# A graph layer on one core: GpSimd's stops between gathers, one in four instead of one in two in the later blocks

## The chip, the core and the metric

The kernel runs on one core of a Trainium2 chip. The core has a matrix engine (TensorE, PE in the profile), a vector engine (VectorE, DVE), a scalar engine (ScalarE, ACT), GpSimd (POOL) and a queue engine (SyncE, SP). They run at the same time and wait for each other by semaphores. Sixteen DMA engines move data between the main memory (HBM) and the on-chip memory (SBUF). The metric is the device time of one execution in microseconds (us), less is better.

## The reference, cut to what matters

```python
def gnn(h, src, dst, rel, norm, bases, w_comp):      # 6250 nodes x 256, 200000 edges sorted by dst, 32 relations, 8 bases
    weight = einsum('rb,bio->rio', w_comp, bases)
    xw = einsum('ni,rio->nro', h, weight)
    msg = xw[src, rel] * norm                        # one row of 256 per edge
    return relu(segment_sum(msg, dst))

def mix(x, ...):      # linear attention over all nodes: K'V summed over all, then per node
    ...               # msg = Q KV Z, @ Wm, layernorm, concat with x, @ W1, relu, @ W2, layernorm, x + msg

def ffn(x, ...):      # 8 experts, all of them for every node, weighted by a softmax router
    ...               # per expert: relu(bn(x W1)), relu(bn(h W2)), h Wo; sum_e w_e y_e

xn = layernorm(x)
x = x + gnn(xn, ...) + mix(xn, ...)
out = x + ffn(layernorm(x), ...)
```

## The kernel before, in words

**The edge part.** The 200000 edges are cut into chunks of 128 (one per partition). A *step* takes one chunk: a gather brings the 128 source rows of 256 floats from `normed_nodes` (`xnD`) into one of the 16 slots of a ring in SBUF, and TensorE multiplies the slot by a selection matrix (`steps(...)` on GpSimd issues the gather, `step(it, k)` on TensorE multiplies: four matmuls of 128x128 per step, tile `PS<-steps`). VectorE adds each step's product to the running sums (line 1433), and SyncE stores them four steps at a time to `step_sums` in HBM (line 546). Sixteen steps make an *iteration*; there are 123 of them, 1968 steps and so 1968 gathers. In the trace all tensors carved from the big buffer are called `steps`.

**The ring.** The gather for a slot may start once TensorE has done the step that used the slot 16 steps earlier: GpSimd waits on `mm_done`. TensorE waits, in front of every even step, on `row_in`, which counts the landing of that step's and the next step's gather, and on `acc_done`, which tells that VectorE has taken the sums two steps back.

**The stretches.** Iterations 0 to 16 carry the first mix pass (keys, values, queries, the first half of W1 for three node tiles of 128 each). Four iterations have steps only. Then three tiles of the second mix pass take two iterations each, and from iteration 27 on the work is cut into *blocks* of eight iterations. Block 0 has steps, the second mix pass for the next block's tiles (`mixing`) and the combination of step sums with the bases (`combine`, matmuls `PS<-bases_s,feed`). Blocks 1 to 11 have these and the eight experts for the tiles of the block before (`first`, `second`, `third`: `PS<-x1t_high,split_in` and the like). After the last step the experts of the last tiles run alone.

**The order of work.** Each engine's program is written out by hand; at each step number fixed pieces of mixing, combining and expert work stand between the steps. TensorE, VectorE and ScalarE take them strictly in that order, so TensorE that waits for a gather holds up all that stands behind it. The eight reads of step sums that a tile's combination needs (`load_agg`, line 576) are issued by SyncE behind the stores of the iteration before; ScalarE reorders them (line 993) for TensorE.

**GpSimd's stops.** GpSimd's only work in the steady stretches is the gathers. In front of some it stops: it writes a small tile `hold` (`memset`, line 796) and waits on the semaphore `held` until that write is done, and only then issues the gather (line 798). Two constants say where:

```python
CALM_END, LIGHT_END = 16, 36
```

In iterations 0 to 15 and 36 to 122 it stops in front of every second gather (16 x 8 + 87 x 8 = 824 stops); in iterations 16 to 35 it never does. Iteration 36 is the second of block 1.

Of the kernel before, what the change touches and what calls it, by code (L numbers as in the profile page):

```python
# [55 lines left out]
UN = 16  # L56
# [24 lines left out]
SETS = 4  # L81
# [8 lines left out]
CALM_END, LIGHT_END = 16, 36  # L90
# [14 lines left out]
def gps_layer(nc, x, src, dst, etype, eweight, bases, w_comp, Wq, Wk, Wv, Wm, W1, W2, g1, b1, g2, b2,  # L105
              Wr, br, fW1, fb1, fg1, fbe1, fm1, fv1, fW2, fb2, fg2, fbe2, fm2, fv2, Wo, bo, out):
    ctx = ExitStack()
    with ctx:
        sems = {}

        def sem(name):
            if name not in sems:
                sems[name] = ctx.enter_context(nc.semaphore(name))
            return sems[name]
# [257 lines left out]
        def wait_apart(eng, name, value):  # L372


            eng.wait_ge(sem(name), value)
            eng.sem_inc(sem("passed"), 1)
# [360 lines left out]
        def _(pool):  # L737
# [50 lines left out]
            pool.wait_ge(sem("rels_out1"), 16)  # L788
            pool.wait_ge(sem("ln_st"), 16 * (LG + 1))

            def steps(it, u, calm=None):
                pool.wait_ge(sem("idx_ready"), it + 1)
                for k in range(UN):
                    wait_apart(pool, "mm_done", it * UN + k + 1)
                    if calm is not None and k % 2 == 0:
                        pool.memset(hold[:, :], 0.0).then_inc(sem("held"), 1)  # L796
                        wait_apart(pool, "held", calm * (UN // 2) + k // 2 + 1)
                    pool.indirect_dma_start(out=ring[:, k, :], out_offset=None, in_=xnD,  # L798
                                            in_offset=bass.IndirectOffsetOnAxis(ap=idxc[:, u, k:k + 1], axis=0)
                                            ).then_inc(sem(f"row_in{k // 2}"), 16)  # L800

            for it in range(ITERS):
                if it < CALM_END:
                    steps(it, it % SETS, it)
                elif it < LIGHT_END:
                    steps(it, it % SETS)
                else:
                    steps(it, it % SETS, it - LIGHT_END + CALM_END)

        @block.scalar  # L810
        def _(act):
# [1430 lines left out]
```

## Time and profile before

| | us |
| --- | --- |
| median of 3 runs | 3474.31 |
| lowest, highest | 3462.02, 3476.06 |
| the profiled execution | 3473.02 |
| its span, first to last instruction | 3471.2 |
| mean granted TensorE clock | 0.947 |
| PE busy | 2978.8 (86%) |
| DVE busy | 2236.0 (64%) |
| POOL busy | 2061.6 (59%) |
| ACT busy | 1001.9 (29%) |

Busy is the time in which an engine executed something of the program; waits and the handling between instructions are not in it. The profile names for each idle stretch what ended it ("<-"); "issue" means that it saw nothing that ended it. GpSimd's spans are rough, so its pace is better read from one start to the next.

### The profile page before, as it was taken

Reading aid. Unit: us, or ns where it says so; the run is one execution under the profiler, and the core shown is the slowest. Engines: PE = TensorE matmul, PEld = TensorE weight load, DVE = VectorE, ACT = ScalarE, POOL = GpSimd, SP = SyncE. Lnnn points to the kernel's source line nnn. Section 1 sums busy time; section 2 is a strip of 40 time slices with the busy share of each in tenths; the row PEclk is TensorE's granted clock in tenths of the full one; section 3 lists DMA queues with packets and bytes.
Section 4 is the critical chain, followed back from the end, with each engine's and each line's share of the span. In section 5 each row is a group of like instructions: output and inputs, shape, how many; then the busy total and the mean of one; then the engine's idle time right before and its main releaser. Section 6 shows DMA issues by size and latency. Waiting matters only on the chain.

```text
span 3471.2 us, 60187 instructions
## 1 busy us (share of the span) xinstructions
PE 2978.8 (86%) x17948; PEld 2616.7 (75%) x17948; DVE 2236.0 (64%) x5966; ACT 1001.9 (29%) x1702; POOL 2061.6 (59%) x2827
## 2 busy tenths in 40 slices
PE   0599996565769989999999999999999999999888
PEld 0477875555658878888887888878888888878778
DVE  4566666455557767777677776766767676767633
ACT  0433331000103333233333333333333333323244
POOL 1466666666566666666666666666666666666600
PEclk9999998678879999999999999999999999999999
DMA  7799987666668888787888878888887888878744
GB/s 179 246 295 294 297 290 234 204 190 201 204 206 267 256 261 266 239 274 244 264 258 258 267 241 266 254 260 255 260 265 247 263 256 268 266 239 274 228 151 144
DMA packets 638070, 852.74 MB, mean 246 GB/s; under 512 B 63579, under 2 KB 515497, under 8 KB 637607
## 3 DMA queue, kind: packets, MB, share of 16 engines
q1 hardware_dynamic: 495087, 536.50, 47.9%
q0 software_dynamic: 95776, 262.27, 26.2%
q10 hardware_dynamic: 46872, 50.02, 4.3%
q8 instruction: 147, 2.41, 0.3%
q14 instruction: 188, 1.54, 0.1%
HBM read 542.52 MB, written 314.58 MB: 247 GB/s over the span
## 4 chain that ended last, share of the span: by engine, by line
PE 58%; issue 13%; DVE 11%; DMA 6%; POOL 4%; another core or an unknown queue 4%; ACTq 2%; ACT 1%; DVEq 0%; SPq 0%; POOLq 0%; PEld 0%; PEldq 0%
PE PS L1850 57%; DMA steps<-normed_nodes,steps 5%; DVE steps L1433 4%; POOL steps L798 4%; DVE h_low L1096 1%; PE PS L1920 1%; DVE feed L1096 1%; DVE steps L1387 1%; ACTq L815 1%; DMA step_sums<-steps 0%; DVE feed L1764 0%; ACT feed L852 0%; DVE steps L1151 0%; POOL hold L796 0%
## 5 line engine op out<-in xcount | busy, mean ns | idle before, releaser
L798 POOL DMA_INDIRECT steps<-normed_nodes,steps x1968 | 1942.1, 987 | 1122.3 <-issue 566.5
L1433 DVE SCALAR_TENSOR_TENSOR steps<-steps,PS 128x256 f32<-128x256 f32 x1968 | 942.5, 479 | 839.7 <-PE PS L1850 478.7
L1850 PE MATMUL PS<-steps 128*128 128x128 f32 x7872 | 1201.3, 291 | 270.3 <-issue 107.1
L1850 PEld LDWEIGHTS PS<-steps 128*128 128x128 f32 x7872 | 1106.2, 203 | 369.3 <-issue 270.9
L1850 PE MATMUL PS<-bases_s,feed 128*128 128x256 f32 x1568 | 370.0, 379 | 2.3 <-issue 2.3
L986 ACT ACTIVATE feed<-PS,bnc 128x512 f32<-128x512 f32 (+1 forms) x416 | 307.4, 751 | 173.4 <-PE PS L1850 141.8
L1387 DVE TENSOR_TENSOR steps<-steps 128x512 f32<-128x512 f32 x495 | 330.0, 687 | 4.3
L1850 PEld LDWEIGHTS PS<-bases_s,feed 128*128 128x128 f32 x1568 | 286.6, 190 | 37.6 <-issue 3.1
L1850 PE MATMUL PS<-w_one,feed 128*128 128x256 f32 (+1 forms) x980 | 295.1, 433 | 2.2 <-issue 2.2
L985 ACT ACTIVATE h_high<-PS,bnc 128x512 fp32r<-128x512 f32 (+1 forms) x208 | 156.7, 753 | 453.1 <-PE PS L1850 313.3
L993 ACT COPY feed<-feed 128x1024 f32<-128x1024 f32 x98 | 205.4, 2096 | 198.0 <-DMA feed<-step_sums 169.2
L1850 PE MATMUL PS<-h_high,split_in 128*128 128x512 f32 (+1 forms) x832 | 247.7, 421 | 11.2 <-ACT feed L986 11.2
L1850 PE MATMUL PS<-x1t_high,split_in 128*128 128x512 f32 (+1 forms) x832 | 236.4, 406 | 0.0
L1850 PEld LDWEIGHTS PS<-w_one,feed 128*128 128x128 f32 x980 | 175.1, 194 | 43.0 <-issue 30.0
L1850 PE MATMUL PS<-w_zero,feed 128*128 128x256 f32 x784 | 196.6, 386 | 4.0 <-DVE feed L1096 3.5
L1764 DVE SCALAR_TENSOR_TENSOR feed<-PS,rw,feed 128x256 f32<-128x256 f32 x392 | 169.8, 475 | 31.7 <-PE PS L1850 31.5
L943 ACT COPY mixbuf<-PS 128x256 f32<-128x256 f32 x49 | 18.3, 373 | 578.5 <-issue 267.2
L1850 PEld LDWEIGHTS PS<-h_high,split_in 128*128 128x128 f32 x832 | 149.2, 199 | 35.1 <-ACT feed L986 13.7
L1850 PEld LDWEIGHTS PS<-feed,w_one 128*128 128x128 f32 x1176 | 149.4, 194 | 27.3 <-issue 27.3
L1096 DVE TENSOR_TENSOR h_low<-feed,h_high 128x512 fp32r<-128x512 f32 (+1 forms) x208 | 129.1, 656 | 48.5 <-ACT feed L986 48.5
L1850 PE MATMUL PS<-feed,w_one 128*128 128x128 f32 x1176 | 157.5, 277 | 0.7 <-issue 0.7
L1850 PEld LDWEIGHTS PS<-x1t_high,split_in 128*128 128x128 f32 x832 | 144.0, 192 | 15.7
(229 smaller groups left out, 2959.4 us busy)
## 6 DMA issues: line engine op xcount, KB each, us to landing
step_sums<-steps SPq DMA_DIRECT2D x492, 512.0 KB
split_in<-expert_split SPq DMA_DIRECT2D x104, 1024.0 KB
feed<-step_sums SPq DMA_DIRECT2D x392, 128.0 KB
steps<-step_types SPq DMA_DIRECT2D x126, 256.0 KB
steps<-normed_nodes,steps POOLq DMA_INDIRECT x1968
w_zero<-in_L_ffn_Wo_dram SPq DMA_DIRECT2D x52, 256.0 KB
w_one<-in_L_ffn_Wo_dram SPq DMA_DIRECT2D x52, 256.0 KB
mixbuf<-mix_hidden SPq DMA_DIRECT2D x50, 256.0 KB
```

The costliest lines, as they stand in the source:

```text
L798: pool.indirect_dma_start(out=ring[:, k, :], out_offset=None, in_=xnD, in_offset=bass.IndirectOffsetOnAxis(ap=idxc[:, u, k:k + 1], axis=0) ...
L815: act.dma_start(lnx[g][:, 0:LT, :], x[nodes_at(g), :].rearrange("(t p) n -> p t n", p=P)).then_inc(sem(f"ln_ld{g}"), 16)
L943: act.copy(mst[:, :, :].rearrange("p k n -> p (k n)"), bank(B_MIX, 0, C)).then_inc(sem("m2_mt"), 1)
L985: act.activation(h1_high[:, k, 0:w], bank(b0 + k, 0, w), ACT.Relu, bias=bias, scale=scale)
L986: act.activation(o[:, k, 0:w], bank(b0 + k, 0, w), ACT.Relu, bias=bias, scale=scale).then_inc(sem(f"f_h{s}"), 1)
L993: act.copy(agg[:, h, :, :], at_nodes[:, h, :, :]).then_inc(sem("b_agg"), 1)
L1096: return dve.tensor_tensor(o, a, b, op)
L1387: dve.tensor_tensor(selm[:, q, :, :, :], hot[:, s, :].unsqueeze(3).to_broadcast([P, BATCH, GN, BASES]), coef[:, s, :].unsqueeze(2).to_broa ...
L1433: dve.scalar_tensor_tensor(acc[:, k % ACCR, :], acc[:, (k - 1) % ACCR, :], keepc[:, k:k + 1], PS[:, a:a + C], ALU.mult, ALU.add).then_inc( ...
L1764: dve.scalar_tensor_tensor(oacc[:, j, :], o_part(j), rw[:, EXPERTS * j + e:EXPERTS * j + e + 1], oacc[:, j, :], ALU.mult, ALU.add).then_in ...
L1850: return pe.matmul(o, a, b, start=start, stop=stop)
L1920: last = pe.transpose(o[:, h * P:(h + 1) * P], frm[:, h * P:(h + 1) * P], ident[:, :])
```

## The change

`steps` on GpSimd gets the distance between two stops as an argument, and the count of stops made before the iteration as another. Iterations 0 to 15 keep a stop in front of every second gather, iterations 16 to 35 keep none, and iterations 36 to 122 now have one in front of every fourth: 16 x 8 + 87 x 4 = 476 stops.

```diff
-            def steps(it, u, calm=None):
+            def steps(it, u, calm=None, apart=2):
                 pool.wait_ge(sem("idx_ready"), it + 1)
                 for k in range(UN):
                     wait_apart(pool, "mm_done", it * UN + k + 1)
-                    if calm is not None and k % 2 == 0:
+                    if calm is not None and k % apart == 0:
                         pool.memset(hold[:, :], 0.0).then_inc(sem("held"), 1)
-                        wait_apart(pool, "held", calm * (UN // 2) + k // 2 + 1)
+                        wait_apart(pool, "held", calm + k // apart + 1)
...
                 if it < CALM_END:
-                    steps(it, it % SETS, it)
+                    steps(it, it % SETS, it * (UN // 2))
                 elif it < LIGHT_END:
                     steps(it, it % SETS)
                 else:
-                    steps(it, it % SETS, it - LIGHT_END + CALM_END)
+                    steps(it, it % SETS, CALM_END * (UN // 2) + (it - LIGHT_END) * (UN // 4), 4)
```

On GpSimd, where iteration 35 goes over into 36, the order before is this (the first line holds the last two gathers of iteration 15 and the 320 of iterations 16 to 35):

```order
L798 DMA steps<-normed_nodes,steps 128x256 x322
L796 MEMSET hold 128x8
L798 DMA steps<-normed_nodes,steps 128x256 x2
L796 MEMSET hold 128x8
L798 DMA steps<-normed_nodes,steps 128x256 x2
L796 MEMSET hold 128x8
```

and after the change, at the same place:

```order
L798 DMA steps<-normed_nodes,steps 128x256 x322
L796 MEMSET hold 128x8
L798 DMA steps<-normed_nodes,steps 128x256 x4
L796 MEMSET hold 128x8
L798 DMA steps<-normed_nodes,steps 128x256 x4
L796 MEMSET hold 128x8
```

What moved: every second `hold` of this stretch is gone, nothing else.

On GpSimd within the blocks, with what each instruction waits for, around the start of an iteration (the wait on `idx_ready`), before:

```order
L798 DMA steps<-normed_nodes,steps 128x256 [waits mm_done]
L796 MEMSET hold 128x8 [waits mm_done]
L798 DMA steps<-normed_nodes,steps 128x256 [waits held]
L798 DMA steps<-normed_nodes,steps 128x256 [waits mm_done]
L796 MEMSET hold 128x8 [waits idx_ready,mm_done]
L798 DMA steps<-normed_nodes,steps 128x256 [waits held]
```

and after:

```order
L796 MEMSET hold 128x8 [waits mm_done]
L798 DMA steps<-normed_nodes,steps 128x256 [waits held]
L798 DMA steps<-normed_nodes,steps 128x256 [waits mm_done] x3
L796 MEMSET hold 128x8 [waits idx_ready,mm_done]
L798 DMA steps<-normed_nodes,steps 128x256 [waits held]
```

What moved: of four gathers, three now wait for `mm_done` alone and one for `held`, where it was two and two. The instructions of TensorE, VectorE, ScalarE and SyncE stand in the same order as before.

## Rows read from the trace of the kernel before

**Rows 1.** Busy time by stretch; columns as in the first line.
```profile
core 0: us, PE busy (x) PEld busy (x) DVE busy (x) ACT busy (x) POOL busy (x), PEclk, DMA share, GB/s
200.00:600.00 400.00, 345.14 (x2423) 293.46 (x2422) 251.90 (x586) 114.88 (x351) 256.09 (x351) 0.94 0.87 282
1100.00:1220.00 120.00, 115.28 (x733) 105.47 (x732) 88.45 (x254) 37.54 (x62) 78.35 (x111) 0.99 0.84 264
1240.00:1280.00 40.00, 34.03 (x191) 28.92 (x190) 28.99 (x84) 14.84 (x20) 25.11 (x38) 0.93 0.87 279
1280.00:1380.00 100.00, 97.52 (x584) 86.64 (x582) 66.68 (x183) 32.31 (x44) 65.47 (x94) 1.00 0.85 262
1284.00:2929.00 1645.00, 1563.22 (x9348) 1371.37 (x9347) 1154.63 (x3126) 529.30 (x755) 1069.44 (x1531) 0.98 0.83 258
3300.00:3471.00 171.00, 146.15 (x721) 130.94 (x719) 54.62 (x142) 76.52 (x114) 0.00 (x0) 0.96 0.46 148
```

**Rows 2.** GpSimd's groups, 1284 to 2929 us.
```profile
L798 POOL DMA_INDIRECT steps<-normed_nodes,steps x1021 | 1008.2, 987 | 576.1 <-issue 300.7 <-PE PS L1850 168.9 <-POOL hold L796 103.8
L796 POOL MEMSET hold<- 128x8 f32 x510 | 62.8, 123 | 0.2
```

**Rows 3.** GpSimd in order of time, in a block: start, us, what.
```profile
2006.80 0.95 POOL L798 DMA_INDIRECT steps<-normed_nodes,steps  x1 [0.79 <-issue]
2008.06 0.95 POOL L798 DMA_INDIRECT steps<-normed_nodes,steps  x1 [0.30 <-issue]
2009.01 0.12 POOL L796 MEMSET hold<- 128x8 f32 x1
2009.91 0.95 POOL L798 DMA_INDIRECT steps<-normed_nodes,steps  x1 [0.79 <-POOL hold L796]
```

**Rows 4.** GpSimd in order of time, in the stretch without stops.
```profile
702.05 0.95 POOL L798 DMA_INDIRECT steps<-normed_nodes,steps  x1 [2.71 <-PE PS L1850]
703.30 0.95 POOL L798 DMA_INDIRECT steps<-normed_nodes,steps  x1 [0.30 <-issue]
704.56 0.94 POOL L798 DMA_INDIRECT steps<-normed_nodes,steps  x1 [0.30 <-issue]
705.80 0.95 POOL L798 DMA_INDIRECT steps<-normed_nodes,steps  x1 [0.30 <-PE PS L1850]
```

**Rows 5.** TensorE's groups, 1284 to 2929 us.
```profile
L1850 PE MATMUL PS<-steps 128*128 128x128 f32 x4084 | 596.5, 281 | 70.0 <-issue 32.8 <-DMA steps<-normed_nodes,steps 26.9 <-DVE steps L1433 8.4
L1850 PE MATMUL PS<-bases_s,feed 128*128 128x256 f32 x1020 | 241.2, 379 | 0.0
```

**Rows 6.** GpSimd and TensorE in order of time, around one stop of TensorE.
```profile
1241.07 0.95 POOL L798 DMA_INDIRECT steps<-normed_nodes,steps  x1 [0.79 <-POOL hold L796]
1242.32 0.94 POOL L798 DMA_INDIRECT steps<-normed_nodes,steps  x1 [0.30 <-issue]
...
1244.09 0.52 PEld L1850 LDWEIGHTS PS<-steps 128*128 128x128 f32 x4 [3.04 <-issue]
1244.12 0.68 PE L1850 MATMUL PS<-steps 128*128 128x128 f32 x4 [2.67 <-issue]
```

**Rows 7.** TensorE's groups, 1100 to 1220 us.
```profile
L1850 PE MATMUL PS<-steps 128*128 128x128 f32 x334 | 48.9, 282 | 3.3 <-DVE steps L1433 2.3 <-issue 1.0
```

**Rows 8.** Waits of ScalarE: us in total, times, longest; 1898 to 3134 us.
```profile
ACT feed L993 <- DMA feed<-step_sums: 65.6, 13, 11.1
```

**Rows 9.** The same in block 0, 837 to 1050 us.
```profile
ACT feed L993 <- DMA feed<-step_sums: 19.4, 2, 14.2
```

**Rows 10.** Clock and DMA by slices of the span (40 equal ones), from the page.
```profile
PEclk9999998678879999999999999999999999999999
DMA  7799987666668888787888878888887888878744
```

## The prediction

> **What bounds the kernel now.** I read the slices of the page first, then busy time by stretch, then GpSimd alone, and last what TensorE stops for. The slices show that the clock sags only between slices 7 and 12, which the change doesn't touch, and is at 9 in all the blocks, with the DMA engines at 7 to 8 tenths [rows 10]. So the change acts in a stretch that looks full of TensorE work. From 1284 to 2929 us, which is eight blocks, TensorE is busy for 1563.22 of 1645 us: 205.6 us a block, 195.4 of them busy, 10.2 idle [rows 1].
>
> GpSimd looks idle there (1069.44 of 1645 us), and isn't. Its 1021 gathers take 1008.2 us, its 510 stops 62.8, and 576.1 us of idle time stand in front of gathers [rows 2]. In order of time this idle time is two fixed pieces: 0.30 us in front of a gather without a stop, 0.79 behind a stop, whatever releaser is named [rows 3]. Half the gathers have each: 510 x (0.79 + 0.30) = 556 us. Of 1645 us only 576 - 556 = 20 are left in which GpSimd waited for somebody, 1.2%. So `mm_done`, the ring's own brake, hardly ever holds it: it issues at its own pace, and that pace is the blocks' pace. A pair of gathers takes 2009.91 - 2006.80 = 3.11 us, 64 pairs take 199 us, and with the longer ones (mean 987 ns against the usual 950) and the 20 us it comes to 205.6.
>
> TensorE pays for it in front of steps: 70.0 us of its 81.8 idle us stand before the matmuls `PS<-steps`, 26.9 put down to the gather's DMA, 32.8 to "issue", 8.4 to VectorE [rows 5]. I count "issue" as gathers too, from the stop at 1244: the two gathers that this step needs were issued at 1241.07 and 1242.32 and ended on GpSimd at 1243.26, and the weights are loaded 0.83 us later, after 3.04 us of idle time for which no releaser is named [rows 6]. So 59.7 us in 1645 are waits for a gather, 3.6%.
>
> The counterproof is the beginning of block 1, where the stretch without stops has left GpSimd ahead: from 1100 to 1220 us the idle time before steps is 3.3 us, none of it put down to a gather and most to VectorE [rows 7].
>
> **The change, part by part.** It removes 87 x 4 = 348 stops from iterations 36 to 122. Each takes 0.12 us for the write and 0.79 - 0.30 = 0.49 us more of idle time, 0.61 us together [rows 3]. That gathers without stops follow each other at the short distance is seen directly, 703.30 to 704.56 to 705.80, 1.25 us [rows 4]. So four gathers take 2 x 3.11 - 0.61 = 5.61 us in place of 6.22, an iteration loses 4 x 0.61 = 2.4 us of GpSimd time and a block 19.5. GpSimd's own pace becomes 205.6 - 19.5 = 186 us a block, and 348 x 0.61 = 212 us of its time go in all. None of this is yet the kernel's time: 186 us lie below TensorE's 195.4 busy us, so TensorE becomes what is late, and only its stops can be won.
>
> Term 1, the stops. GpSimd still has its lead at 1220 us [rows 7], TensorE stops for gathers from 1240 on [rows 6], and the steps end at about 3300, as GpSimd's empty last stretch shows [rows 1]: 2080 us from 1220, of which 3.63% (59.7 / 1645) are waits for gathers, 75 us. With 9 us a block to spare, 16 slots are refilled after a slow gather, and the waits should go nearly all. Bounds: 0 if the waits are of another kind than I take them for, -75 if all go. I take -75, because GpSimd's spare time is larger than the waits.
>
> Term 2, the clock. After a cluster of stops TensorE's granted clock falls from its upper level (2.4 GHz) to its lower (1.2): the stretch 1240 to 1280, with 6 us idle, has 0.93, the one behind it, with 2.5 in 100, has 1.00 [rows 1]. A mean of 0.98 in the blocks means 4% of the time at the lower level, 83 us of 2080. At most half of it, 42 us, is lost work. Part of these falls come without a gather's stop, and not all work scales with the clock. Bounds 0 and -42, and I take -10, near the lower one. The Trainium skill, TensorE: Matmul & The Clock Gate, Part 1, says that the throttled state is the default and activity releases it. The trace agrees in the direction (0.93 beside 1.00). By the rule taken strictly, blocks without stops stay at 1.00, and this term is the whole of it; that is the third rival.
>
> Term 3, what comes to light. A stop for a gather also gives VectorE and ScalarE time to catch up. Where GpSimd was ahead, from 1100 to 1220, TensorE was still idle for 4.72 of 120 us, 3.9% [rows 1], half of it before steps on VectorE's sums [rows 7]. In the steady blocks the idle time that is not a gather's is 81.8 - 59.7 = 22.1 us, 1.3%. If it rises to 3.9%, 2.6% of 2080 us come back, 54 us. Bounds 0 and +54. Block 1 follows a disturbed stretch and is one sample, so I take half, +27.
>
> The stops in iterations 0 to 15 stay, and nothing upstream of iteration 36 changes: 0. The removed write goes to a tile of 128x8 that nobody reads: 0. The tail after 3300 us is TensorE and ScalarE alone and has no gathers: 0. No DMA is added or removed, they only come up to 5% denser, which is the second rival.
>
> Sum: -75 - 10 + 27 = -58 us. Against the profiled execution's 3473.0 us (span 3471.2 and 1.8 around it) that is 3415 us. The median of the runs shown, 3474.3, is 1.3 above the profiled one, so I leave it at 3415, 1.7% less than before. By the ends of the terms the range of this case is 3473 - 117 = 3356 to 3473 - 21 = 3452.
>
> **The rivals.**
>
> The first: the stops go, but other waits take their place, and the time stays, 3466 us (3456 to 3490). The hand-written order has hops through VectorE and ScalarE (`mixing`, line 1433, the experts' hidden rows) that are timed by TensorE's passing; term 3 is then at its full 54, the clock gives nothing, and some 15 us of gather waits stay: -75 + 15 + 54 = -6. For it speaks block 1, where an idle share of 3.9% stood with no gather late. Against it: the blocks from 1284 on have only 1.3% of such idle time. That the change doesn't do what it says ends here too: if the freed 0.49 us were not idle time but the descriptor work of the gather before, GpSimd's pace would stay and so would the time. The 1.25 us between gathers without stops [rows 4] speak against that.
>
> The second, on the other side: transfers collide, 3520 us. The place is the read of the step sums for a tile's combination. ScalarE already waits for it, 65.6 us in 13 waits in six blocks of 24 tiles, the longest 11.1 [rows 8], and in block 0, without stops, 19.4 us in only two waits, the longest 14.2 [rows 9]. TensorE has cover today: 0.0 us idle before `PS<-bases_s,feed` [rows 5]. With gathers issued in longer runs beside stores and reads, at a DMA share of 0.83 in the blocks where the first mix pass has 0.87 [rows 1], these reads land later; once the cover is used up, each us per tile costs 43 us over the 43 tiles of blocks 1 to 11. At 2.5 us a tile it is 107, less the 58 won: +49, 3522. It decides from 1.4 us a tile beyond the cover, and shows as slower from 1.8. Against it: once the ring is full, gathers are issued at TensorE's pace, not in longer runs. The Trainium skill, DMA: Bandwidth & Descriptors, Queues, rings and completion order, says that each DMA engine takes turns between its queues by packets, which would let a run of gathers push SyncE's reads back. No row here shows the turns themselves, only the share of 0.83.
>
> The third: the clock stays up and nothing comes to light, -75 - 42 = -117, 3356 us. For it: the stretch at 1280 to 1380 with 2.5% idle and a clock of 1.00. Against it: such stretches are short, and in block 1 TensorE stops for VectorE though no gather is late [rows 7].
>
> **How the numbers follow.** The forecast has 0.47, the third rival 0.11, the first 0.23, the second 0.19. What a measurement of this kernel can tell from no change is about 0.5%, 17 us, so 3457 to 3491 is the same. The forecast and the third rival are faster, and 0.02 of the first at its lower edge: 0.60. Same is 0.22, with the rest of the first and a little of the second. Slower is 0.18. The range must reach up into the second rival for its cheaper half and down to the third: 3350 to 3500 leaves out some 0.05 below and 0.11 above. The forecast's own range is 3356 to 3452.
>
> **What would show it.** In the profile of the changed kernel: 476 stops on line 796; GpSimd's idle time before gathers in the blocks with waits of 1 us and more for TensorE, a sign that the ring is full; the idle time before `PS<-steps` from 70 us in eight blocks to under 25, with VectorE's line 1433 as its first releaser; a block in about 200 us in place of 205.6; the clock in the blocks at 0.99. Wrong I am if blocks still take 205 us: with the idle time before steps gone and other idle time in its place it is the first rival, with ScalarE's waits on `feed<-step_sums` doubled and idle time before `PS<-bases_s,feed` the second, and with GpSimd still never waiting its pace was not what I took it for.

## The result, and the profile after

| | before | changed |
| --- | --- | --- |
| median, us | 3471.32 (4 runs, 3462.02 to 3476.06) | 3606.15 (4 runs, 3586.7 to 3614.09) |
| profiled execution's span | 3471.2 | 3584.9 |
| mean granted TensorE clock | 0.947 | 0.937 |
| POOL busy | 2061.6 | 2017.8 |
| stops | 824 | 476 |

The changed kernel is slower: 1.0376 of before, 95% interval 1.0347 to 1.0406. The forecast was 3415 us with a range of 3350 to 3500, so the sign is wrong and the time lies outside the range. The profiled execution of the changed kernel was the fastest of its four: the two spans differ by 113.7 us, the medians by 134.8.

The page after: the clock by slices [rows 10], the chain that ended last, and the group of the steps on TensorE.

```profile
PEclk9999997677879999999999999999999999999999
PE 64%; DVE 13%; issue 10%; another core or an unknown queue 7%; DMA 2%; ACT 2%; ACTq 2%; POOL 1%; SPq 1%; DVEq 0%; POOLq 0%; PEld 0%; PEldq 0%
L1850 PE MATMUL PS<-steps 128*128 128x128 f32 x7872 | 1211.0, 292 | 259.9 <-DVE steps L1433 158.9
```

The clock sags in the same slices as before. Where TensorE stops in front of steps, it now waits for VectorE, not for gathers. The chain has 7% of "another core or an unknown queue" in a program that runs on one core. Time by stretch: iterations 16 to 35, and eight whole blocks (from the first step of block 2).

```profile
core 0: us, PE busy (x) PEld busy (x) DVE busy (x) ACT busy (x) POOL busy (x), PEclk, DMA share, GB/s
567.70:1075.40 507.70, 328.99 (x1818) 297.08 (x1818) 292.44 (x759) 47.12 (x85) 311.72 (x324) 0.76 0.69 203
1263.20:3001.40 1738.20, 1593.72 (x9378) 1392.41 (x9377) 1161.25 (x3134) 532.14 (x760) 1036.15 (x1277) 0.97 0.78 245
```

The same eight blocks of before, cut at the same instructions, and of GpSimd and TensorE the groups in the eight blocks after, which answer to [rows 2, 5]:

```profile
1244.10:2895.00 1650.90, 1570.24 (x9377) 1377.81 (x9377) 1157.73 (x3132) 533.62 (x760) 1072.50 (x1535) 0.98 0.82 258
L1850 PE MATMUL PS<-steps 128*128 128x128 f32 x4097 | 598.9, 282 | 72.5 <-issue 33.5 <-DMA steps<-normed_nodes,steps 27.4 <-DVE steps L1433 9.7
```

```profile
L796 POOL MEMSET hold<- 128x8 f32 x256 | 30.0, 117 | 105.3 <-issue 71.4 <-PE PS L1850 30.5 <-remote 3.0
L1850 PE MATMUL PS<-steps 128*128 128x128 f32 x4097 | 602.9, 283 | 59.2 <-DVE steps L1433 49.5 <-issue 8.7
L1850 PE MATMUL PS<-bases_s,feed 128*128 128x256 f32 x1024 | 243.1, 380 | 0.3 <-issue 0.3
L1850 PE MATMUL PS<-h_low,split_in 128*128 128x512 f32 x256 | 103.1, 454 | 38.7 <-issue 19.3 <-DVE h_low L1096 14.7
L1850 PE MATMUL PS<-w_s,mixbuf 128*128 128x256 f32 x257 | 66.8, 405 | 24.0 <-ACT mixbuf L961 23.9
L1850 PE MATMUL PS<-wm_s,mixbuf 128*128 128x256 f32 x128 | 34.6, 393 | 10.8 <-issue 10.0 <-ACT mixbuf L943 0.6
```

A block takes 1738.2 / 8 = 217.3 us, before 206.4. GpSimd does what was foretold: in front of `hold` it now waits 105.3 us (before 0.2), so the ring is full, and of TensorE's 60.9 us of gather waits (33.5 + 27.4, with "issue" counted as gathers) some 9 are left. But TensorE is idle for 144.5 us against 80.7, in front of steps on VectorE's sums (49.5 against 9.7), on `h_low` (before 4.8), `w_s` (0.6) and `wm_s` (0.9).

Why these come late shows in the waits of the other engines. Those put down to "remote", a releaser that the profile doesn't see, of 5 us or more in the eight blocks:

```profile
ACT h_high L985 <- remote: 58.6, 12, 8.1
DVE steps L1433 <- remote: 51.3, 18, 5.0
ACT feed L986 <- remote: 49.7, 21, 4.1
ACT mixbuf L955 <- remote: 49.1, 15, 4.2
ACT feed L1001 <- remote: 44.1, 8, 6.1
DVE mixbuf L1096 <- remote: 39.8, 8, 7.3
ACT mixbuf L943 <- remote: 30.5, 3, 11.7
POOL steps L798 <- remote: 30.0, 22, 2.0
DVE feed L1764 <- remote: 9.6, 9, 2.0
```

With the small ones they are 371 us; in the same blocks of before 43 (23.8 of it at L943 and 11.3 at L1433). These are whole waits, summed over three engines that can wait at the same time; they are not lateness alone, and not time of the kernel. Nearly all of these instructions wait for a semaphore of TensorE. One case in order of time, start and length:

```profile
1570.85 1.14 PE L1850 MATMUL PS<-steps 128*128 128x128 f32 x8
1571.83 0.38 PE L1920 MATMUL PS<-ident,mixbuf 128*128 128x128 f32 x2
1572.05 1.06 PE L1850 MATMUL PS<-steps 128*128 128x128 f32 x8
1572.86 1.18 PE L1850 MATMUL PS<-h_high,split_in 128*128 128x512 f32 x4
1574.76 0.95 POOL L798 DMA_INDIRECT steps<-normed_nodes,steps  x1 [0.79 <-issue]
1574.88 0.99 DVE L1433 SCALAR_TENSOR_TENSOR steps<-steps,PS 128x256 f32<-128x256 f32 x2 [3.20 <-remote]
1574.92 0.81 ACT L955 ACTIVATE mixbuf<-PS,gb 128x128 f32<-128x128 f32 x2 [3.22 <-remote]
1575.79 1.29 DVE L1096 TENSOR_TENSOR h_low<-feed,h_high 128x512 fp32r<-128x512 f32 x2
1576.53 0.80 PE L1850 MATMUL PS<-h_low,split_in 128*128 128x512 f32 x1 [2.49 <-issue]
```

VectorE waits for the first group of step products, which ends at 1571.99, and ScalarE for the transposes, which end at 1572.21. Both start at 1574.9, 2.9 and 2.7 us later, though TensorE itself had gone on to the next steps and to `h_high` at once. The trace also keeps when each semaphore was updated: for these two it has 1574.86 and 1574.90, just before the two engines start. Then VectorE's `h_low` is late, and TensorE stands for 2.49 us. The Trainium skill, Perfetto Trace Analysis, Tensor Engine Instruction (MATMUL, LD_WEIGHTS), says that the end shown for a matmul is estimated, and that its semaphore is pushed only after PSUM (the memory that matmuls write to) has acknowledged the write and seen by others later still; a bar can so be over while its semaphore is not yet out. The trace agrees: the update stands 2.87 us behind the end of the bar here, and 0.01 us at the same place in the second group's trace.

So the trace shows TensorE's work seen late. It doesn't show why. It has a second oddity: of the 1968 updates of the steps' semaphore it holds 1540, and the first trace of before 1332; between 1572.00 and 1574.86 it has none by any engine, not even that of `hold`, though GpSimd passed its wait on it at 1574.01. With updates missing, the sums under "remote" are no full account. Starts and ends of instructions are, and they are counted below.

The first question was whether the change brings this on every chip.

### The profile page after: what moved, and what is told of

It reads as the page before. It is cut to its first block, busy times and chain, and to the rows that moved or that the text cites. A ratio compares the mean times of both kernels' runs of the same rounds, so it can differ in the third digit from the quotient of the medians.

```text
span 3584.9 us, 59491 instructions
## 1 busy us (share of the span) xinstructions
PE 3017.8 (84%) x17948; PEld 2646.3 (74%) x17948; DVE 2241.9 (63%) x5966; ACT 999.8 (28%) x1702; POOL 2017.8 (56%) x2479
## 4 chain that ended last, share of the span: by engine, by line
PE 64%; DVE 13%; issue 10%; another core or an unknown queue 7%; DMA 2%; ACT 2%; ACTq 2%; POOL 1%; SPq 1%; DVEq 0%; POOLq 0%; PEld 0%; PEldq 0%
PE PS L1850 62%; DVE steps L1433 5%; DVE h_low L1096 2%; PE PS L1920 1%; DMA steps<-normed_nodes,steps 1%; DVE steps L1387 1%; POOL steps L798 1%; DVE feed L1764 1%; ACTq L815 1%; DVE feed L1096 1%; SPq L576 0%; PE PS L1958 0%; DMA feed<-step_sums 0%; ACT h_high L985 0%
## 5 line engine op out<-in xcount | busy, mean ns | idle before, releaser
L1433 DVE SCALAR_TENSOR_TENSOR steps<-steps,PS 128x256 f32<-128x256 f32 x1968 | 943.1, 479 | 904.6 <-PE PS L1850 601.4
L1850 PEld LDWEIGHTS PS<-steps 128*128 128x128 f32 x7872 | 1121.2, 205 | 343.7 <-issue 296.1
L1850 PE MATMUL PS<-w_one,feed 128*128 128x256 f32 (+1 forms) x980 | 303.4, 443 | 2.2 <-issue 2.2
L1850 PE MATMUL PS<-h_low,split_in 128*128 128x512 f32 (+1 forms) x416 | 156.6, 434 | 53.6 <-issue 24.6
L943 ACT COPY mixbuf<-PS 128x256 f32<-128x256 f32 x49 | 18.3, 373 | 612.2 <-PE PS L1920 314.1
L1850 PEld LDWEIGHTS PS<-h_low,split_in 128*128 128x128 f32 x416 | 82.8, 200 | 110.0 <-DVE h_low L1096 62.1
```

Of the source, the lines that this page charges most:

```text
L943: act.copy(mst[:, :, :].rearrange("p k n -> p (k n)"), bank(B_MIX, 0, C)).then_inc(sem("m2_mt"), 1)
L1433: dve.scalar_tensor_tensor(acc[:, k % ACCR, :], acc[:, (k - 1) % ACCR, :], keepc[:, k:k + 1], PS[:, a:a + C], ALU.mult, ALU.add).then_inc( ...
L1850: return pe.matmul(o, a, b, start=start, stop=stop)
```

## The experiments

The runs came to four chips, one for each group below; each group has its own runs of before, 7 in number. The results carry the numbers of these four, but not of the chip of the first measurement. I call that one the first chip; that it is a fifth, and not one of the four in another state, rests on its times alone.

### First group: the stops alone

Three theories. *Run*: lateness (of a semaphore behind the end of its matmul) grows with the gathers that GpSimd issues behind one another. *Ring*: what counts is that GpSimd catches up and waits on TensorE. *Chain*: the first rival of the prediction, the order's hops through VectorE and ScalarE. All edits are in the call of `steps` for iterations 36 on (`times=2` makes each stop twice; `near` lets a gather start only that many steps later, so that it is 6 steps ahead of TensorE and not 16):

```diff
four_two_stops:  steps(it, it % SETS, 4, times=2)
two_near:        steps(it, it % SETS, 2, near=10)
none:            steps(it, it % SETS, 0)
everywhere:      steps(it, it % SETS, 2)     # and in iterations 16 to 35 too
```

**four_two_stops.** 

> The changed kernel (a stop in front of every fourth gather in iterations 36 to 122), but each of these stops is made twice in a row, so that GpSimd's own pace is again about that of before (5.6 us for four gathers plus some 0.6 to 0.9 for the second stop, against 6.2 before) and it hardly ever waits for the ring. The symptom in the changed kernel is that VectorE, ScalarE and GpSimd together see TensorE's semaphore some us after its matmul (waits of these engines that the profile puts down to 'remote'). Theory run: this comes from four gathers in a row without a stop between them; then it stays here, with 'remote' waits of VectorE's line 1433 at 20 us and more in eight blocks, and a time of 3530 to 3620 us. Theory ring: it comes from GpSimd standing at its wait for TensorE because the ring is full; then it is gone, with the time at 3460 to 3500 us. Theory chain: there is no late semaphore, TensorE's other waits only came to light when the gathers were early; then the time is that of before too, 3460 to 3500, since the gathers are as late as before.

**two_near.** 

> The kernel before (a stop in front of every second gather), but in iterations 36 to 122 a gather may start only when TensorE has done the step 6 before it in place of 16 before it: GpSimd then often waits for TensorE, in runs of two gathers at most. Theory run: no late semaphores; the time rises only by the smaller buffer, which catches less of TensorE's unevenness: 3500 to 3600 us, idle time of TensorE before steps put down to gathers, 'remote' waits of line 1433 as small as before (about 10 us in eight blocks). Theory ring: the late semaphores come here too, 'remote' waits of line 1433 at 20 us and more in eight blocks. The time alone does not tell the two apart, the releasers do.

**none.** 

> No stop at all in iterations 36 to 122 (the first mix pass keeps every second): the dose. Theory run: longer runs, later semaphores, clearly slower than the changed kernel, 3650 to 3850 us, 'remote' waits larger than in it. Theory ring: the ring is full as in the changed kernel, so about its time, 3590 to 3640. Theory chain: the same, 3590 to 3640, with little in 'remote'.

**everywhere.** 

> The kernel before with a stop in front of every second gather in iterations 16 to 35 as well, where it has none. In that stretch of the kernel before VectorE's line 1433 has large 'remote' waits. Theories run and ring: they go (GpSimd at its own pace of 25.7 us an iteration does not run ahead), and the 20 iterations, 25.3 us each before, now take GpSimd's own 25.5 to 26.5, so the time is within 25 us of before, 3465 to 3500. Theory chain: the waits stay, since they come from the long chain of the mix pass, and the gathers' slower pace is added: 3500 or more.

| before here 3375.88 us | us | of before |
| --- | --- | --- |
| four_two_stops | 3257.41 | 0.9641 (0.9621 to 0.9662) |
| two_near | 3714.7 | 1.1001 (1.0972 to 1.1031) |
| none | 3240.72 | 0.9598 (0.9582 to 0.9615) |
| everywhere | 3476.02 | 1.0298 (1.028 to 1.0316) |

Every theory missed `none`: fewer stops made the kernel faster, and there is no "remote" wait in its trace. `four_two_stops` lies below all of its ranges and `two_near` above its own, though by its releasers, with no "remote" wait, it fits theory run. `everywhere` lies in its range by luck: the range stood for "within 25 us of before", and before itself takes 3376 us here, 2.7% less than on the first chip. `two_near` shows what the ring's depth is worth. Its eight blocks:

```profile
1173.30:3072.30 1899.00, 1641.11 (x9377) 1422.92 (x9377) 1163.92 (x3135) 532.46 (x760) 1062.23 (x1536) 0.95 0.72 224
L1857 PE MATMUL PS<-steps 128*128 128x128 f32 x4097 | 628.2, 290 | 257.1 <-issue 150.4 <-DMA steps<-normed_nodes,steps 89.7 <-DVE steps L1394 15.6
```

A shorter lead turns into waits for gathers, 240.1 of the 257.1 us before steps (150.4 + 89.7). `everywhere` takes 511.4 us for iterations 16 to 35, where before, without stops there, takes 411.4 on the next group's chip: that, too, is GpSimd's pace with stops (160 pairs of gathers at 3.11 us are 498). None of this tells yet whether the variants differ from the changed kernel in kind or the chips do.

### Second group: the changed kernel again

**The changed kernel, nothing altered.** 

> The changed kernel once more, nothing altered. It was 3.8% slower than before where it was measured first, but three of four variants on another chip showed that stops taken out make the kernel faster there, and in their traces no engine ever waited on a semaphore of TensorE that came late. Theory chip: two chips differ in whether TensorE's semaphores are seen late while GpSimd gathers in long runs. On a chip where the kernel before takes about 3376 us, the changed kernel should then take 3240 to 3265 us (ratio 0.96 to 0.967), with hardly any wait put down to 'remote' on VectorE's line 1433 and ScalarE's line 955. On one where before takes about 3471 us, it should be 3600 us again (1.035 to 1.040). Rival, theory variant: the variants differ from the changed kernel in some other way than the stops, and the changed kernel is slower on every chip: over 3450 us where before takes 3376.

**The kernel before, for its trace.** 

> The kernel before, for its trace on the same chip. If it takes about 3376 us, theory chip expects that its stretch without stops (iterations 16 to 35) is shorter than in the first trace of before, and that its blocks are as long as there, 205 to 206 us, since GpSimd's pace sets them on both chips. If it takes about 3471 us the first trace should come again. The rival (the two chips differ in the pace of every engine) expects the whole program shorter by the same 2.8%, blocks of 200 us.

**none again.** 

> No stop in iterations 36 to 122, as in none, for a comparison on this chip. Where before takes 3376 us, 3240 us again, equal to the changed kernel within 0.7%, since TensorE sets the pace in both. Where before takes 3471 us: theory run (the lateness grows with the number of gathers that GpSimd issues behind one another without a stop) expects it slower than the changed kernel, 3640 to 3800 us; theory ring (a stop has no part in it, what counts is that GpSimd catches up with TensorE and waits on its semaphore) expects it equal to the changed kernel within 1%, 3570 to 3640.

**four_two_stops again.** 

> A stop at every fourth gather, made twice, as in four_two_stops: the number of stops of before, the run length of the changed kernel. Where before takes 3376 us, 3257 us again (ratio 0.96 to 0.97). Where before takes 3471 us: theory run expects lateness as in the changed kernel and the time between, 3550 to 3620 us; theory ring expects GpSimd to fill the ring still, if more slowly, and the same range; only if the total time in stops counts and not their spacing is it at 3460 to 3480.

| before here 3384.57 us | us | of before |
| --- | --- | --- |
| changed | 3245.0 | 0.9581 (0.9561 to 0.96) |
| none | 3242.56 | 0.9577 (0.9561 to 0.9593) |
| four_two_stops | 3258.64 | 0.9627 (0.9611 to 0.9643) |

All four came out as theory chip expected. The same kernel that lost 3.8% in the first measurement gains 4.2% in this one. So it is not the program that differs but the chip, or its state at the time; the two can't be told apart, since nothing was run again where semaphores are late. Before on this chip, iterations 16 to 35 and the eight blocks, and its steps in the blocks:

```profile
545.50:956.90 411.40, 289.06 (x1817) 262.08 (x1818) 290.17 (x757) 45.40 (x83) 313.12 (x321) 0.87 0.82 249
1144.00:2791.80 1647.80, 1570.08 (x9377) 1383.24 (x9377) 1158.53 (x3135) 533.21 (x760) 1068.78 (x1535) 0.98 0.82 258
L1850 PE MATMUL PS<-steps 128*128 128x128 f32 x4097 | 604.0, 283 | 72.5 <-DMA steps<-normed_nodes,steps 41.9 <-issue 23.7 <-DVE steps L1433 2.7
```

Before on the first chip, iterations 16 to 35, with its "remote" waits there:

```profile
567.50:1070.10 502.60, 323.63 (x1820) 293.50 (x1818) 291.71 (x759) 45.36 (x83) 310.39 (x323) 0.78 0.68 203
DVE steps L1433 <- remote: 90.0, 26, 8.4
PE PS L1850 <- DVE steps L1433: 85.2, 39, 12.2
ACT mixbuf L943 <- remote: 64.0, 5, 14.9
POOL steps L798 <- remote: 54.4, 30, 3.0
ACT mixbuf L955 <- remote: 24.4, 4, 6.7
DVE mixbuf L1096 <- remote: 19.8, 6, 6.2
```

The blocks of before are alike on both chips, 1650.9 and 1647.8 us. The stretch without stops is not: 502.6 against 411.4, 91 of the 103 us between the two spans. There the first chip has 261.5 us of "remote" waits, the second group's chip none, and TensorE waits for VectorE's sums 85.2 us against 26.5.

The starts of instructions show the same without any semaphore record. The table counts VectorE's pairs (line 1433) that start more than 0.5 us behind both the end of their step products and the end of VectorE's instruction before, and, of all pairs, the sum of what goes beyond 0.1 us:

| | iterations 16 to 35, 160 pairs | eight blocks, 512 pairs |
| --- | --- | --- |
| before, first chip | 48, 122.9 us | 14, 16.7 us |
| changed, first chip | 55, 129.9 us | 98, 136.5 us |
| before, second group's chip | 1, 1.5 us | 0, 0.4 us |
| changed, second group's chip | 1, 2.7 us | 0, 0.6 us |

So VectorE is late on the first chip wherever GpSimd gathers without stops or with few, in before already, and seldom where it stops at every second gather. The changed kernel on the second group's chip, its eight blocks, steps, and the same place in the program as the case above:

```profile
1129.30:2708.80 1579.50, 1544.98 (x9378) 1359.15 (x9377) 1158.53 (x3137) 532.23 (x760) 1049.47 (x1286) 0.99 0.85 270
L1850 PE MATMUL PS<-steps 128*128 128x128 f32 x4097 | 581.5, 277 | 14.4 <-DVE steps L1433 10.1 <-issue 1.9 <-DVE steps L1387 1.1
L1850 PE MATMUL PS<-h_low,split_in 128*128 128x512 f32 x256 | 99.8, 434 | 4.0 <-DVE h_low L1096 0.3
...
1410.53 1.14 PE L1850 MATMUL PS<-steps 128*128 128x128 f32 x8
1411.50 0.38 PE L1920 MATMUL PS<-ident,mixbuf 128*128 128x128 f32 x2
1411.70 1.00 DVE L1433 SCALAR_TENSOR_TENSOR steps<-steps,PS 128x256 f32<-128x256 f32 x2 [0.34 <-PE PS L1850]
1411.92 0.81 ACT L955 ACTIVATE mixbuf<-PS,gb 128x128 f32<-128x128 f32 x2 [0.55 <-PE PS L1920]
```

VectorE's pair starts 0.03 us after the step products' end (1411.67) and ScalarE 0.04 after the transposes' (1411.88); on the first chip 2.9 and 2.7 us.

### Third group: lags made by hand

If late starts are enough for the loss, a lag put in by hand on a chip without them must bring a loss. (A lag is a row of small writes, each of which waits for the one before.) The edit is in VectorE's `pair(it, p)`, behind its wait for `mm_done`:

```diff
+                if it >= LIGHT_END and p == 3 * it % 8:
+                    for _ in range(15):
+                        lagged[0] += 1
+                        dve.memset(idle[:, :], 0.0).then_inc(sem("lagged"), 1)
+                        wait_apart(dve, "lagged", lagged[0])
```

**The changed kernel with lags.** 

> The changed kernel with one artificial lag of about 3 us on VectorE in each of the iterations 36 to 122 (87 of them, 15 small dependent writes behind VectorE's wait for TensorE's step products, in front of a pair of line 1433): some 24 us of lag a block, about what TensorE's late semaphores brought in the first trace of the changed kernel (12 us in 100). On a chip where before takes about 3380 us, theory late (late semaphores at VectorE are by themselves enough for the 20 us a block between the changed kernel's two measurements, 216 and 197 us) expects +10 to +20 us a block, so 3360 to 3470 us. The rival, theory more (the lag at VectorE is mostly hidden by TensorE's other work, and the loss on the first chip came from the lag on ScalarE or something else) expects less than +5 us a block, 3245 to 3300. On a chip where before takes 3471 us it should be slower than the changed kernel, over 3650 us by theory late.

**The kernel before with lags.** 

> The kernel before with the same 87 lags. GpSimd sets its pace, with 10 us a block to spare on TensorE, and its ring holds 16 rows. Theory late expects that it bears part of them: +5 to +14 us a block, so 3430 to 3530 us where before takes 3380, and a loss smaller than the changed kernel's by 3 to 10 us a block; theory more expects no loss, 3380 to 3400 us. If it loses exactly as much as the changed kernel, then a lag in VectorE stops GpSimd too, and the stops were no cover for it.

**No stop anywhere** (iterations 0 to 15 too). 

> No stop anywhere, those of the first mix pass (iterations 0 to 15) left out too. Where before takes 3380 us and no semaphore comes late: iterations 0 to 15 lose 16 x 8 stops of 0.61 us of GpSimd time, 78 us, of which TensorE stops for gathers there for perhaps a quarter; I expect 3200 to 3240 us, faster than none's 3242. Against it: GpSimd's gathers there would take DMA time from the loads of the first mix pass, then 3240 to 3290. Where before takes 3471 us: theory run (lateness in long runs of gathers) expects the same lateness as in iterations 16 to 35 in the first 16 too, 3650 to 3850 us; theory ring expects 3570 to 3660.

| before here 3378.81 us | us | of before |
| --- | --- | --- |
| changed, lags | 3519.05 | 1.0422 (1.0405 to 1.044) |
| before, lags | 3512.5 | 1.0405 (1.0388 to 1.0423) |
| no stops | 3200.21 | 0.9473 (0.9453 to 0.9493) |

A lag is 15 writes 0.245 us apart, 3.7 us, 29 a block. Eight blocks of the changed kernel with lags, and its steps; then of before with lags:

```profile
1144.50:2918.60 1774.10, 1614.41 (x9378) 1417.92 (x9377) 1222.23 (x4099) 533.47 (x760) 1042.10 (x1281) 0.95 0.77 240
L1858 PE MATMUL PS<-steps 128*128 128x128 f32 x4097 | 619.6, 288 | 114.5 <-DVE steps L1441 113.2
```

```profile
1146.30:2914.30 1768.00, 1610.46 (x9378) 1415.98 (x9377) 1220.77 (x4101) 533.94 (x760) 1075.43 (x1541) 0.95 0.77 241
L1858 PE MATMUL PS<-steps 128*128 128x128 f32 x4097 | 620.9, 289 | 115.3 <-DVE steps L1441 113.9
```

The changed kernel goes from 197.4 us a block to 221.8, more than the 10 to 20 expected and more than the first chip's 217.3; before goes from 206.0 to 221.0. With lags the two take the same time to within 0.2%, and the clock is 0.95 in both. Of the changed kernel's 4.2% nothing is left: the stops cost nothing where TensorE waits for VectorE anyway. That prices lateness, and tells where the gain goes. The dose is larger than on the first chip, where VectorE's pairs are late by 136.5 / 8 = 17.1 us a block and not by 29; the next group has a smaller one. And it makes the two kernels equal, not the changed one slower; for that the lateness must be in the changed kernel and not in before, as the first chip's traces have it (136.5 us in eight blocks against 16.7).

`no_stops` is the fastest kernel of this study where no semaphore is late.

### Fourth group: size, place, engine

**The changed kernel with 7 writes in place of 15.** 

> The changed kernel with the same 87 lags on VectorE, at less than half the size: 7 dependent writes of 0.245 us, 1.7 us each, 13.7 us a block (changed_lag had 15, 3.7 us, 29.4 a block, and lost 24.7 us a block or 274 us in all). If the loss is in proportion, 128 us: 3370 to 3380 us where before takes 3380, no gain left. If TensorE has cover for short lags (it works ahead of VectorE by a bank or two) it is under 60 us: below 3305. On the chip where semaphores come late, over 3650 us.

**Before with lags in iterations 16 to 35 alone** (the condition is `CALM_END <= it < LIGHT_END and p in (1, 4, 6)`). 

> The kernel before with lags of 3.7 us on VectorE in its stretch without stops only (iterations 16 to 35, three in each, 60 lags, 220 us in all, which is what I read from the first trace as late semaphores there: 218 us). Theory late: this by itself brings before from 3380 to about 3470 us, the first chip's time, since that stretch was 91 us longer there (502.6 against 411.4) and the rest of the program within 12 us; I expect 3440 to 3500. The rival (the light stretch is slower on the first chip for another reason, the pace of TensorE or the DMA) expects less than +40 us, under 3420.

**The changed kernel with the lag on ScalarE** (the loop stands in `hidden`, behind the wait for `f_l1`, with 8 small copies). 

> The changed kernel with a lag on ScalarE instead, 8 dependent copies of some 0.4 us, about 3.3 us, in front of the first hidden activations of each expert's first layer (8 in a block, 104 in all). By theory late ScalarE's hops are a way for the loss as well, h_low and w_s waits were part of the first trace: +5 to +20 us a block, 3300 to 3460 us where before takes 3380. The rival, that only VectorE's sums count, expects under +3 us a block, below 3280.

**no_stops with the lags of the third group.** 

> no_stops (3200 us, the fastest so far) with the 87 lags of 3.7 us. If a lag costs the same wherever GpSimd is ahead, +274 us: 3470 to 3480 us, and it stays 40 us ahead of changed_lag (3519) only by the first mix pass. If stops in the blocks were of any use under lags, it is slower than changed_lag: over 3530.

| before here 3373.33 us | us | of before | lag in all, us | loss, us |
| --- | --- | --- | --- | --- |
| changed, small lags | 3334.27 | 0.9877 (0.9854 to 0.99) | 149 | 100 |
| before, lags in 16 to 35 | 3527.08 | 1.0447 (1.0419 to 1.0476) | 220 | 151 |
| changed, lags on ScalarE | 3354.0 | 0.993 (0.9904 to 0.9956) | 244 | 118 |
| no stops, lags | 3481.13 | 1.0309 (1.0282 to 1.0337) | 320 | 282 |

The loss is the ratio less that of the same kernel without lags (0.9581, 1, 0.9581, 0.9473), times 3373; ScalarE's 832 copies took 159.9 us and 84.0 us of gaps between them, 2.3 us a lag and not 3.3. Small lags lose two thirds of their length, large ones nine tenths (320 us of lag cost the changed kernel 284 in the third group); so the first lay between its two cases. `no_stops` loses as much as the changed kernel, to within 2 us: the stops that the changed kernel keeps are no cover against a lag.

ScalarE is a second way for the loss, by the table at half the length; but not all of it is lost in the blocks. The eight blocks with small lags on VectorE are the first line, with lags on ScalarE the second:

```profile
1135.50:2777.60 1642.10, 1562.84 (x9378) 1365.99 (x9378) 1185.73 (x3584) 532.24 (x760) 1043.00 (x1281) 0.99 0.83 259
1133.20:2753.00 1619.80, 1548.02 (x9378) 1372.48 (x9378) 1162.22 (x3137) 626.31 (x1272) 1044.56 (x1283) 0.99 0.83 263
```

With ScalarE's lags they take 1619.8 us, 40 more than the changed kernel's 1579.5, for 150 us of lag; that is a quarter. And behind the last step, where the experts run alone, 16 lags (38 us) lengthen the end from 170.5 to 217.0 us.

**How much of the first chip's blocks this explains.** The eight blocks with small lags take 1642.1 us, 7.8 a block above those without, for 13.7 us of lag; with large ones it was 24.3 for 29.4. The 17.1 us a block by which VectorE's pairs are late on the first chip lie between; in proportion they cost some 11 us, an estimate from these two runs. The changed kernel's blocks took 217.3 - 197.4 = 19.9 us more there. So VectorE's late sums account for somewhat over half of it; the rest is not priced, and the late starts of ScalarE and GpSimd are in it.

Lags in iterations 16 to 35 lengthen that stretch of before by 161 us (against the second group's trace), more than the first chip's 91 and more than expected, but by the same picture, a low clock and steps that wait for VectorE:

```profile
547.70:1120.60 572.90, 359.02 (x1819) 329.78 (x1819) 350.10 (x1659) 46.50 (x84) 319.06 (x338) 0.72 0.62 186
L1858 PE MATMUL PS<-steps 128*128 128x128 f32 x1280 | 260.5, 374 | 186.0 <-DVE steps L1441 185.5
```

The rival, that such lags would cost under 40 us, is out. But these were 220 us by hand, and the first chip's pairs are late by 122.9 us in this stretch; in proportion that makes 90 us, an estimate, of the 91 to be explained. So, by that estimate, the lateness that is seen is about enough for the first chip's time of before. A slower pace of gathers or DMAs as a part of it was not tried.

**What stays open.** No trace of the four groups has a single "remote" wait, so nothing was tried where semaphores are late. That the distance between stops decides how often it is late there rests on the traces of two kernels on one chip, not on an experiment; theories run and ring were never told apart. Nor is it shown what holds a semaphore back. In the case above VectorE and ScalarE are released within 0.04 us of each other, 0.12 us behind the start of a gather; whether that is chance wasn't tried. The updates that the first chip's traces lack may be another sign of the same trouble or a fault of the recording alone. All times here are of executions whose span and clock were recorded, so it isn't shown either that the lateness is there without it.

## Why the prediction was wrong, point by point

**GpSimd's pace**: right, on every chip. With the ring full it waits in front of `hold`.

**The terms in eight blocks.** Each difference between two traces is taken times 2080 / 1645, for the prediction's stretch. "Gather" is issue and DMA before steps, "other" the rest of TensorE's idle time.

| | forecast | first chip | second group's chip |
| --- | --- | --- | --- |
| term 1, gather waits | -75 | -52.2, so -66 | -63.7, so -81 |
| term 2, TensorE's busy time | -10 | +23.5, so +30 | -25.1, so -32 |
| term 3, other waits | +27 | +116.0, so +147 | +20.5, so +26 |
| sum | -58 | +111 | -87 |

The sum of +111 answers to the 113.7 us between the two spans. Term 1 was right on both chips. Term 3 is the step that failed. It was sized from the idle time of block 1, with 54 us as its upper bound, as if VectorE and ScalarE were late only by their own work. On the first chip it came to 147 us. The bound priced waits that stay equally long and come to light; it left out waits that become longer, because TensorE's work is seen late. Term 2 went with it: more idle time, a clock of 0.97 in place of 0.98, and 23.5 us more busy time.

**The row that was not read.** It is in the first trace of before: in iterations 16 to 35, a stretch with longer runs of gathers than the change makes, VectorE waits 90.0 us in 26 times for "remote" releasers, and TensorE 85.2 us for VectorE. The prediction saw the low clock there [rows 10] and passed on, as the change doesn't touch the stretch. It read GpSimd's pace without stops from it [rows 4], but not what the other engines did meanwhile. That stretch was a trial of the change that the trace of before already held.

**Where no semaphore is late.** On the second group's chip the sign was right and the size too small: -58 forecast, -118 between the two spans (3368.6 and 3250.3) and -140 between the medians (3384.6 and 3245.0; the profiled run of before was the fastest there). Terms 1 and 3 fit. Term 2 was three times as large. And block 1 gains 21 us more (iterations 36 to 42: 187.1 against 166.4 us), which the prediction excluded since GpSimd "still has its lead" there [rows 7]. It had this lead because the first chip's stretch before was slow: on the second group's chip TensorE waits 20.7 us for gathers in these seven iterations of before, on the first at most 4.2.

**The range.** The prediction gave term 1 the bounds 0 and -75, but "by the ends of the terms" it went from 3356 to 3452, with term 1 at -75 at either end. With its 0 the upper end is 3473 + 54 = 3527. The measured time lies above that too.

**The rivals.** The first (other waits take the place of gathers) named the right place, VectorE's and ScalarE's hops, and the wrong price, at most 54 us, so it ended at no change. The second, transfers that collide, had the right sign by another mechanism, and is out: before `PS<-bases_s,feed` TensorE is idle for 0.3 us. ScalarE's waits for the step sums grow from 95.3 to 113.1 us in the eight blocks, no doubling, and on the second group's chip, where the kernel got faster, from 110.1 to 173.3. The third (the clock stays up, nothing comes to light) comes nearest where semaphores are in time: -117 forecast, -118 between the spans, though -140 between the medians and by another split, since 26 us did come to light.

## What to carry to other kernels

If a kernel holds back one engine, look in the trace for a stretch where it doesn't, and read there what all the others wait for, above all waits whose releaser the profile can't name: what the change would bring was already in the trace. Price new slack twice, once with the other waits as they are and once with them longer. And a gain of some per cent by timing alone should be measured on more than one chip, and with before beside it each time, before it is called one: here it was 0.958 on one and 1.038 on another, for the same program.

## What the runs showed of the hardware

- One program took 3471 us in one measurement and 3373 to 3385 on four chips in others, 2.5 to 2.8% less, though its blocks take 1650.9 and 1647.8 us on the first and on one of the four; most of the difference (91 of 103 us) is in one stretch.
- On one chip VectorE, ScalarE and GpSimd saw TensorE's finished matmuls up to several microseconds late (2.9 us in the case shown; VectorE's sums by 136.5 us in eight blocks), where GpSimd issued gathers with few stops between; on another, the same place of the same program, 0.03 us.
- The traces of that chip lack semaphore updates: 1332 and 1540 of the steps' 1968 are there, in all others 1954 to 1964.
- A dependent small write on VectorE takes 0.245 us from start to start, so a chain of them is a finely set lag. In this kernel such lags cost 7.8 us a block at 13.7 us a block, and 24.3 at 29.4.
